# Vision layer on one core: image 0 of h is loaded at the end of the token stage, from a ring kept beside the constants

## The chip, the cores and the metric

The kernel is one launch on one core of a Trainium2 chip. The time is the device time of that core in microseconds (us), the median of several executions. Engines: TensorE (PE in the profile; PEld is its weight load), VectorE (DVE), ScalarE (ACT), GpSimd (POOL) and SyncE (SP, which here only issues transfers). Each engine works through its own list in order; semaphores tie the lists together. SP and ACT issue transfers whose descriptors hardware makes; those of POOL are made by software on POOL and put in a scratch area of on-chip memory (SBUF).

## The reference

Cut to what is computed (16 images, 256 tokens each, width 192):

```python
h = tok(x)                              # x [16,3,64,64]
#   three levels p = 1, 2, 4: patches in Hilbert order (a gather), 16 at a time,
#   o_p = patches @ W_p.T + b_p;  levels 2 and 4 interpolated to 256 tokens
#   h = concat(o_1, o_2, o_4) @ Wf.T + bf
h = h + attn(layernorm(h))              # 12 heads of 16, causal
#   q, k, v = layernorm(h) @ w_inp + b_inp
#   qf = (exp(q@omega - diag - max over features) + eps) / 8       (kf: max over heads, features)
#   a = (causal qf . kf . v) / (causal qf . kf + eps);  attn = a @ w_out + b_out
h = h + ffn(layernorm(h))               # 8 experts, 2 chosen by each token
#   probs = softmax(x @ gate_w + gate_b); y = sum over 2 of gelu(x @ w1_e + b1_e) @ w2_e + b2_e
#   + bk_scale * (clip(Green's function of x @ v_w) @ out_w + out_b)
```

## The kernel before

The kernel is three blocks, one after the other. A block has one instruction list for each engine, and the engines meet at its end before the next begins.

**Token stage** (`tokens_block`, 0 to about 84 us). POOL gathers the patches with 42 indirect transfers (L194); PE turns and multiplies them in groups, and DVE and ACT copy the even and the odd groups out of PSUM. The last work is h itself: for each half t of the tokens (t = 0, 1) eight groups of two images, ("h", 8t + n). Their results stand in `hs`. For each quarter q of the images SP waits for its two groups and stores half t of four images to the DRAM tensor `h_dram` (L179), eight stores of 384 KB. The four stores of t = 0 count on the semaphore `h_out[0]`, those of t = 1 on one each, `h_out[1]` to `h_out[4]`. So image 0 is whole in DRAM when all stores of t = 0 and the one of t = 1, q = 0 have landed. After its last store SP has nothing to wait for that is still open, and the block ends.

**Attention stage** (`attention_block`, about 84 to 429 us). The sixteen images go through a pipeline of four steps (`sched`): step `one` of image i, with steps of images i-1, i-2 and i-3 beside it. h of an image is read from `h_dram` into a ring `hb` of four places (192 KB an image, `load_h`, L473), counted by `h_in`. SP's list begins with the waits for `h_out[0]` and `h_out[1]` and with `load_h(0)`; then, for image i, it waits until image i has landed, issues `load_h(i + 1)`, and issues a sixteenth of the second expert weights (`a_raw`, L489). DVE's list begins with `stats1(0)` and `apply1(0)`: the sums of the first layer norm (L831, L834), a wait for POOL's reciprocal root (L519, L521), and the norm applied (L839). POOL's begins with four memsets (L508 to L513). PE's first instruction is the turn of the normed image (L576); ACT copies it out (L797), and the projections follow (L623 and L684). The order of all of this is written out by hand.

**Experts stage** (`experts_block`, about 429 us to the end). For 39 tiles of 256 slots POOL gathers token rows (L1141, 78 transfers) and adds the weighted results into the output (L1153, 78 transfers); eight transfers at the end add the spectral part (L1161). Its constants and the three weight tensors live beside the blocks in SBUF, so their places in memory depend on what stands before them.

Of the kernel before, what the change touches and what calls it, by code (L numbers as in the profile page):

```python
# [25 lines left out]
P = 128  # L26
B, T, D = 16, 256, 192
NT = B * T // P
TJ = T // P
KH = D // 2  # L30
# [7 lines left out]
NE, FF = 8, 768  # L38
# [32 lines left out]
def tokens_block(nc, a, keep, c, h_dram, x2_dram, tbl_dram):  # L71
# [6 lines left out]
    with ExitStack() as ctx:  # L78
        sb = lambda n, s, d=F32: ctx.enter_context(nc.sbuf_tensor("t_" + n, s, d))
# [67 lines left out]
        @block.sync  # L147
        def _(sp):
            sp.dma_start(idx[:], a["idx"].bitcast(U32)).then_inc(idx_in, 16)
            for dst, src in ((w2[:], a["w2"]), (w1[:], a["w1"]), (bias[:], a["tok_b"]), (up2[:], a["up2"]),  # L150
                             (wf02[0:EMB], a["wf"][0:EMB]), (wf02[EMB:P], a["wf"][2 * EMB:]),
                             (wf1[0:EMB], a["wf"][EMB:2 * EMB]), (wf1[EMB:EMB + 1], a["bf"])):
                sp.dma_start(dst, src).then_inc(params_in, 16)
            sp.dma_start(top[0:EMB], a["w0_b0"].unsqueeze(1).broadcast_to([EMB, B, EMB])).then_inc(top_in, 16)
            sp.dma_start(fine[EMB:P], a["up1"].unsqueeze(1).broadcast_to([EMB, B, T])).then_inc(up1_in, 16)
            sp.wait_ge(pads_ready, 3)
            sp.dma_start(tbl_dram.rearrange("(p n) c -> p (n c)", p=P), pads[:].rearrange("p n c -> p (n c)")).then_inc(pads_out, 16)
            sp.dma_start(x2_dram[B * T:].rearrange("(j p) c -> p j c", j=2), no_row[:].unsqueeze(1).broadcast_to([P, 2, XW])).then_inc(pads_out, 16)
            of_expert = lambda rows, e: a["ew1"][rows, 2 * e:2 * e + 2].rearrange("k u f -> k (u f)")
            for e in range(NE):  # L160
                if e == RING:
                    sp.wait_ge(omega_zero, 1)
                    for h in range(HC):
                        sp.dma_start(omega[h * NF:(h + 1) * NF, h, 0:NF], a["omega_t"]).then_inc(att_in, 16)
                    sp.dma_start(wqk_t, a["wqk_t"]).then_inc(att_in, 16)
                    for dst, src in ((c["wqkv"][:, :, 2 * H * HW:], a["wv"]), (c["w_out"][:], a["w_out"]), (c["w_gate"][:], a["w_gate"])):
                        for rows in (slice(0, KH), slice(KH, KH + 1)):
                            sp.dma_start(dst[rows], src[rows]).then_inc(att_in, 16)
                if e >= RING:
                    sp.wait_ge(w1_low, 2 * (e - RING + 1))  # L170
                sp.dma_start(raw_a[:, e % RING], of_expert(slice(0, P), e)).then_inc(raw_in[e % RING], 16)
                for r in (0, EMB):
                    sp.dma_start(raw_b[r:r + EMB, e % RING], of_expert(slice(P, D), e)).then_inc(raw_in[e % RING], 16)
            h_half = h_dram.rearrange("p b (j d) -> p b j d", j=TJ)
            for t in range(TJ):
                for q in range(B // 4):
                    b = slice(4 * q, 4 * q + 4)
                    wait_out(sp, ("h", 8 * t + 2 * q), ("h", 8 * t + 2 * q + 1))
                    sp.dma_start(h_half[:, b, t], hs[:, b, t]).then_inc(h_out[1 + q if t else 0], 16)  # L179
            sp.wait_ge(pads_out, 32)  # L180

        @block.gpsimd
# [201 lines left out]
def attention_block(nc, a, keep, c, h_dram, out, x2_dram, tbl_dram):  # L384
# [11 lines left out]
    with ExitStack() as ctx:  # L396
# [6 lines left out]
        eps_col, eight, region, minus_half, entry = (c[n] for n in ("eps_col", "eight", "region", "minus_half", "entry"))  # L403
        wqkv, w_out, w_gate, h_out = c["wqkv"], c["w_out"], c["w_gate"], c["h_out"]

        hb = sb("hb", [P, 4, TJ, D])
        stats, mv, rstd1 = sb("stats", [P, TJ, 6]), sb("mv", [P, TJ, 2]), sb("rstd1", [P, TJ])
        var_eps = {n: sb("var_eps_" + n, [P, TJ]) for n in ("rstd1_ready", "rstd2_ready")}
        xn = sb("xn", [P, TJ, D])
# [30 lines left out]
        AB = ps("ab", [P, 512])  # L440
        M = ps("misc", [P, 512])

        names = """setup h_in xn_ready xnT_done xnT_out qk_done v_done v_out top_done shift_done
            feat_raw exp_done hi_ready lo_ready qT_done kT_done qf_done qT_out kT_out qf_out state_done state_out
            s_done s_out av_done att_ready attT_done attT_out proj_done h2_ready xn2_ready xn2T_done xn2T_out logit_done
            logit_out found gap_ready prob_ready picked chosen_ready counted slots_ready prefix_done place_step rows_ready
            scattered h2_stored x2_stored cleared tail rstd1_ready rstd2_ready norm_step att_step
            raw_in high low""".split()
        s = {n: sem("b_" + n) for n in names}
        block = ctx.enter_context(nc.Block())  # L450
        SPARE = 4 * P - 2 * VW

# [17 lines left out]
        @block.sync  # L470
        def _(sp):
            def load_h(b):
                sp.dma_start(hb[:, b % 4], h_dram[:, bass.ds(b, 1)].rearrange("p b (j d) -> p (b j) d", j=TJ)  # L473
                             ).then_inc(s["h_in"], 16)

            def emit(i, one, two, tail, choice):
                if one and not (fixed(i) and i == B - 1):
                    if not fixed(i) or i >= 3:
                        sp.wait_ge(s["h2_stored"], 16 * (i - 2))
                        sp.wait_ge(s["xn2_ready"], i - 2)  # L480
                    sp.wait_ge(s["h_in"], 16 * (i + 1))
                    if fixed(i) and i == 3:
                        for q in range(1, B // 4):
                            sp.wait_ge(h_out[1 + q], 16)
                    load_h(i + 1)
                if one:
                    if not (fixed(i) and i == 0):
                        wait_apart(sp, s["low"], i)
                    sp.dma_start(raw[:], a["ew2"][:, bass.ds(i, 1)].rearrange("k u f d -> k (u f) d")).then_inc(s["raw_in"], 16)  # L489
                if tail:  # L490
                    wait_apart(sp, s["h2_ready"], i - 1)
                    sp.dma_start(out_tokens[bass.ds(i - 2, 1)].rearrange("b p j d -> (b p) j d"),
                                 hb[:, (i + 2) % 4]).then_inc(s["h2_stored"], 16)
                    wait_apart(sp, s["xn2_ready"], i - 1)
                    rows = x2_tokens[bass.ds(i - 2, 1)].rearrange("b p j d -> (b p) j d")
                    sp.dma_start(rows[:, :, 0:D], xn2[:]).then_inc(s["x2_stored"], 16)
                    sp.dma_start(rows[:, :, D:XW], xn2[:, :, P:D]).then_inc(s["x2_stored"], 16)
            sp.wait_ge(h_out[0], 16 * (B // 4))
            sp.wait_ge(h_out[1], 16)
            load_h(0)  # L500
            sched(sp, emit)
            sp.wait_ge(s["h2_stored"], 16 * B)
            sp.wait_ge(s["x2_stored"], 32 * B)
# [988 lines left out]
def vit_layer(nc, a, out):  # L1492

    scratch = lambda n, shape: nc.dram_tensor(n, shape, F32).ap()
    h_dram = scratch("h_dram", (P, B, TJ * D))
    x2_dram, tbl_dram = scratch("x2_dram", (B * T + TW, XW)), scratch("tbl_dram", (NSLOT, 2))
    v_dram, g_dram, spec_dram = scratch("v_dram", (NT, P)), scratch("g_dram", (2, B, T)), scratch("spec_dram", (B * T, D))
    with ExitStack() as ctx:
        sb = lambda n, s: ctx.enter_context(nc.sbuf_tensor(n, s, F32))
        ident_r = ctx.enter_context(nc.sbuf_tensor("ident", [P, P], F32R))  # L1500
        count = ctx.enter_context(nc.sbuf_tensor("count", [P, TJ, NE], BF16))
        pot = sb("pot", [P, B, TJ])
        w1 = {n: ctx.enter_context(nc.sbuf_tensor("x_" + n, [P, UNITS, UF], F32R)) for n in ("w1h", "w1l", "w1s")}
        w2s = ctx.enter_context(nc.sbuf_tensor("x_w2s", [P, UNITS, UT, 2 * D], F32R))
        keep = dict(ident_r=ident_r, count=count, pot=pot, w2s=w2s, **w1)
        with ExitStack() as inner:
            sb = lambda n, s, d=F32: inner.enter_context(nc.sbuf_tensor("c_" + n, s, d))
            c = dict(causal=sb("causal", [P, P], BF16), before=sb("before", [P, P], BF16), ones=sb("ones", [P, P], BF16),
                     block_mask=sb("block_mask", [HC * NF, HC, VW], BF16), own_head=sb("own_head", [HC * NF, 2]),
                     eps_col=sb("eps_col", [P, 1]), eight=sb("eight", [P, NE]), region=sb("region", [P, NE]),  # L1510
                     minus_half=sb("minus_half", [P, TJ]), entry=sb("entry", [P, 2, TJ, 2]),
                     wqkv=sb("wqkv", [KH + 1, 2, 2 * H * HW + D]), w_out=sb("w_out", [KH + 1, 2, D]),
                     w_gate=sb("w_gate", [KH + 1, 2, NE + 1]),
                     h_out=[inner.enter_context(nc.semaphore(f"h_out{n}")) for n in range(1 + B // 4)])
            tokens_block(nc, a, keep, c, h_dram, x2_dram, tbl_dram)
            attention_block(nc, a, keep, c, h_dram, out, x2_dram, tbl_dram)
        experts_block(nc, a, keep, x2_dram, tbl_dram, out, v_dram, g_dram, spec_dram)
# [53 lines left out]
```

## Time and profile before

| | us |
|---|---|
| median of 3 runs (812.67, 813.17, 816.4) | 813.17 |
| the profiled execution | 815.63 |
| its span, first to last instruction | 813.8 |
| PE busy | 675.7 (83%) |
| DVE busy | 499.9 (61%) |
| ACT busy | 438.0 (54%) |
| POOL busy | 437.3 (54%) |
| mean granted PE clock | 0.903 |

The profiled execution lies 2.46 us above the median, inside the range of the three runs. Times in a row are microseconds from the start of the span. In a timeline row the first number is the start, the second the length; a merged row (x2, x8) spans several instructions. In brackets stands how long the engine had been idle and what ended that. "PEclk" is the clock that was granted to PE as a share of 2.4 GHz: 1.00 is 2.4 GHz, 0.50 is 1.2 GHz.

### The profile page before, as it was taken

How to read it: one execution, taken by the hardware profiler on the slowest of the kernel's cores; microseconds unless marked ns; L12 is line 12 of the kernel's file. 1: busy time of each engine (PE TensorE's matmuls, PEld its weight loads, DVE VectorE, ACT ScalarE, POOL GpSimd, SP SyncE). 2: the span in 40 equal slices, each digit the busy share in tenths (PEclk: the TensorE clock that was granted, in tenths of full speed). 3: DMA queues.
4: the chain of work that ended last, by engine and by line, in shares of the span. 5: the costliest groups of instructions: out<-in, count | busy, mean ns of one | idle time of the engine just before them, and what ended most of it. 6: DMA issues, size and time to landing. Idle time of an engine off the chain costs nothing. (4 is left out here: it accounts for less than half of the span.)

```text
span 813.8 us, 17136 instructions
## 1 busy us (share of the span) xinstructions
PE 675.7 (83%) x4943; PEld 630.0 (77%) x4944; DVE 499.9 (61%) x1474; ACT 438.0 (54%) x852; POOL 437.3 (54%) x456
## 2 busy tenths in 40 slices
PE   2558489999999999999711899999979999999940
PEld 2328379988898999989611899999979999999940
DVE  1444337777777777776314588887996656656510
ACT  1334246766666666665001677767645665666610
POOL 7771223544555555444234377777765765665442
PEclk9659769999999999999555999999989999999985
DMA  8963302211221223210002143333322343343228
GB/s 206 224 137 98 104 25 55 56 49 47 47 57 47 60 57 61 47 37 24 24 23 45 32 68 56 60 61 57 63 39 47 68 74 77 76 76 78 50 39 155
DMA packets 63713, 55.08 MB, mean 68 GB/s; under 512 B 24345, under 2 KB 55520, under 8 KB 63664
## 3 DMA queue, kind: packets, MB, share of 16 engines
q0 software_dynamic: 19840, 23.53, 17.0%
q1 hardware_dynamic: 39344, 27.76, 14.7%
q10 hardware_dynamic: 4480, 3.21, 1.2%
q8 instruction: 21, 0.34, 0.2%
q14 instruction: 28, 0.23, 0.1%
HBM read 32.52 MB, written 25.10 MB: 71 GB/s over the span
## 5 line engine op out<-in xcount | busy, mean ns | idle before, releaser
L1153 POOL DMA_INDIRECT result<-e_y,e_tag x78 | 139.7, 1791 | 92.8 <-DVE e_y L1483 81.0
L1212 PE MATMUL e_yp<-x_w2s,e_hh 128*128 x468 | 140.9, 368 | 2.3 <-DVE e_y L1483 2.3
L1476 DVE TENSOR_TENSOR e_hl<-e_hid,e_hh 128x512 fp32r<-128x512 f32 x117 | 80.2, 690 | 90.4 <-ACT e_hh L1278 90.2
L534 POOL DMA_INDIRECT tbl_dram<-c_entry,a_slot x64 | 64.4, 1007 | 131.9 <-DVE c_entry L999 112.1
L1270 ACT ACTIVATE e_hid<-e_hidden,e_b 128x256 f32<-128x256 f32 x234 | 101.3, 475 | 54.0 <-PE e_hidden L1199 42.3
L1213 PE MATMUL e_yp<-x_w2s,e_hl 128*128 x468 | 118.2, 253 | 0.0
L616 PEld LDWEIGHTS a_ab<-a_values,a_masked 128*128 128x128 f32 x768 | 98.4, 199 | 13.8 <-issue 13.0
L616 PE MATMUL a_ab<-a_values,a_masked 128*128 (+1 forms) x768 | 103.9, 279 | 5.0 <-DVE a_masked L877 5.0
L1278 ACT CAST e_hh<-e_hid 128x512 fp32r<-128x512 f32 x117 | 72.4, 621 | 62.0 <-PE e_yp L1213 62.0
L1141 POOL DMA_INDIRECT e_x<-x_dram,e_tag x78 | 82.9, 1062 | 40.1 <-issue 21.0
L1212 PEld LDWEIGHTS e_yp<-x_w2s,e_hh 128*128 128x128 f32 x468 | 88.8, 190 | 2.6 <-issue 2.5
L1213 PEld LDWEIGHTS e_yp<-x_w2s,e_hl 128*128 128x128 f32 x468 | 90.5, 193 | 0.0
L1195 PE MATMUL e_hidden<-e_xh,e_w 128*128 128x256 f32 x234 | 73.0, 312 | 15.7 <-DVE e_xl L1347 12.0
L877 DVE TENSOR_TENSOR a_masked<-a_s,c_causal 128x512 f32<-128x512 f32 x96 | 64.6, 684 | 16.4 <-PE a_s L592 15.1
L1197 PE MATMUL e_hidden<-e_xl,e_w 128*128 128x256 f32 x234 | 67.4, 288 | 0.0
L1196 PE MATMUL e_hidden<-e_xh,e_w 128*128 128x256 f32 x234 | 67.4, 288 | 0.0
L1198 PE MATMUL e_hidden<-e_xh,e_w 128*128 128x256 f32 x234 | 67.3, 288 | 0.0
L1199 PE MATMUL e_hidden<-e_xl,e_w 128*128 128x256 f32 x234 | 67.2, 287 | 0.0
L1195 PEld LDWEIGHTS e_hidden<-e_xh,e_w 128*128 128x128 f32 x234 | 45.9, 196 | 20.2 <-issue 13.4
L788 ACT ACTIVATE a_qb_t<-a_fa,c_own_head 96x768 fp32r<-96x768 f32 x64 | 53.9, 893 | 6.8 <-PE a_fa L636 6.8
L527 POOL TENSOR_TENSOR a_split<-a_feat,a_split 128x192 fp32r<-128x192 f32 x64 | 36.6, 591 | 31.6 <-ACT a_split L773 30.3
L623 PE MATMUL a_fa<-c_wqkv,a_xn_t 97*128 97x408 f32 (+1 forms) x128 | 52.6, 535 | 0.9 <-ACT a_xn_t L797 0.9
(250 smaller groups left out, 1545.8 us busy)
## 6 DMA issues: line engine op xcount, KB each, us to landing
a_raw<-in_ew SPq DMA_DIRECT2D x16, 288.0 KB, 3.1
x_w2s<-in_ew SPq DMA_DIRECT2D x8, 384.0 KB, 11.8
x_w2s<-in_ew SPq DMA_DIRECT2D x16, 192.0 KB, 13.1
h_dram<-x_w2s SPq DMA_DIRECT2D x8, 384.0 KB, 2.7
a_hb<-h_dram SPq DMA_DIRECT2D x16, 192.0 KB, 3.4
result<-a_hb SPq DMA_DIRECT2D x16, 192.0 KB, 3.7
x_dram<-a_att SPq DMA_DIRECT2D x16, 192.0 KB, 3.7
spec_dram<-e_space ACTq DMA_DIRECT2D x16, 192.0 KB, 1.9
```

The lines of the kernel that those rows point to most:

```text
L616: last = pe.matmul(beside(o + r * VW), masked[n % 2][:, r], own_and_zeros.unsqueeze(1).broadcast_to([P, 2, 2, VW]), start=n == 0 and r == ...
L1141: pool.indirect_dma_start(out=x[:, i % 2, j], out_offset=None, in_=x2_dram, in_offset=bass.IndirectOffsetOnAxis(ap=tag[:, i % 8, j, 0:1].b ...
L1153: pool.indirect_dma_start(out=out, in_=y[:, j], in_offset=None, out_offset=bass.IndirectOffsetOnAxis(ap=tag[:, i % 8, j, 0:1].bitcast(U32) ...
L1195: pe.matmul(o, w(0), xh[:, 0], start=True, stop=False)
L1196: pe.matmul(o, w(1), xh[:, 0], start=False, stop=False)
L1197: pe.matmul(o, w(0), xl[:], start=False, stop=False)
L1198: pe.matmul(o, w(2), xh[:, 1], start=False, stop=False)
L1212: pe.matmul(Y[:, j, 0:2 * D], hh[:, f, c], w(f, 2 * D), start=f == 0, stop=False, skip_group_check=True)
L1213: last = pe.matmul(Y[:, j, 0:D], hl[:, f, c], w(f, D), start=False, stop=False, skip_group_check=True)
L1270: act.activation(hid[:, f], HID[:, f % 4, f // 4], ACT.Gelu_apprx_tanh, bias=b1[:, bass.ds(e, 1), f]).then_inc(s["hid_ready"], 1)
L1278: act.copy(hh[:, f:f + 2].rearrange("p f t -> p (f t)"), hid[:, f:f + 2].rearrange("p f t -> p (f t)")).then_inc(s["hid_high"], 1)
L1476: g.tensor_tensor(hl[:, f:f + 2].rearrange("p f t -> p (f t)"), hid[:, f:f + 2].rearrange("p f t -> p (f t)"), hh[:, f:f + 2].rearrange("p ...
```

## The change

`hb` and the semaphore `h_in` move from the attention stage to the tensors that both stages share (`c`). In the token stage SP, after the store of t = 1, q = 1, waits for `h_out[0]` and `h_out[1]` and issues the load of image 0; the stores of q = 2 and q = 3 follow behind it. The same two waits and the load go from the head of the attention stage. The ring now takes 6 KB of each partition during the token stage too; the scratch for POOL's descriptors is set to 8192 bytes of a partition, half of the 16384 that it has without the argument.

```diff
@@ tokens_block, SP @@
                     wait_out(sp, ("h", 8 * t + 2 * q), ("h", 8 * t + 2 * q + 1))
                     sp.dma_start(h_half[:, b, t], hs[:, b, t]).then_inc(h_out[1 + q if t else 0], 16)
+                    if t and q == 1:
+                        sp.wait_ge(h_out[0], 16 * (B // 4))
+                        sp.wait_ge(h_out[1], 16)
+                        sp.dma_start(c["hb"][:, 0], h_half[:, 0]).then_inc(c["h_in"], 16)
             sp.wait_ge(pads_out, 32)
@@ attention_block @@
-        hb = sb("hb", [P, 4, TJ, D])
+        hb = c["hb"]
...
-        names = """setup h_in xn_ready ...
+        names = """setup xn_ready ...
         s = {n: sem("b_" + n) for n in names}
+        s["h_in"] = c["h_in"]
...
-            sp.wait_ge(h_out[0], 16 * (B // 4))
-            sp.wait_ge(h_out[1], 16)
-            load_h(0)
             sched(sp, emit)
@@ vit_layer @@
-                     w_gate=sb("w_gate", [KH + 1, 2, NE + 1]),
+                     w_gate=sb("w_gate", [KH + 1, 2, NE + 1]), hb=sb("hb", [P, 4, TJ, D]),
+                     h_in=inner.enter_context(nc.semaphore("h_in")),
@@ kernel @@
-    nc = bacc.Bacc("TRN2", target_bir_lowering=False, num_devices=1)
+    nc = bacc.Bacc("TRN2", target_bir_lowering=False, num_devices=1, dynamic_dma_scratch_size=8192)
```

On SP's list the end of the token stage and the head of the attention stage stand thus before (L179 the stores of h, L78 the end of the block, L473 the loads of h, L489 the expert weights):

```order
L179 DMA h_dram<-x_w2s 128x4x192 x8
L78 UNCONDITIONAL_BRANCH
L470 UNCONDITIONAL_BRANCH
L473 DMA a_hb<-h_dram 128x384 x2
L489 DMA a_raw<-in_ew 128x576
L473 DMA a_hb<-h_dram 128x384
L489 DMA a_raw<-in_ew 128x576
```

And now, at the same place on SP (L183 is the new load, L478 and L494 are the old L473 and L489):

```order
L179 DMA h_dram<-x_w2s 128x4x192 x6
L183 DMA c_hb<-h_dram 128x384
L179 DMA h_dram<-x_w2s 128x4x192 x2
L78 UNCONDITIONAL_BRANCH
L475 UNCONDITIONAL_BRANCH
L478 DMA c_hb<-h_dram 128x384
L494 DMA a_raw<-in_ew 128x576
L478 DMA c_hb<-h_dram 128x384
L494 DMA a_raw<-in_ew 128x576
```

One load has moved from behind the block's end to between the sixth and the seventh store; of the two loads that stood at the head of the attention stage one is left. The lists of the other four engines are the same, line numbers apart.

## Rows read from the trace of the kernel before

**Rows 1.** Waits from 84 to 120 us: engine, line, releaser; total us, times, longest.

```profile
PE a_fa L576 <- DVE a_xn L839: 7.2, 1, 7.2
```

**Rows 2.** Timeline, all engines, from the block's start to the projections.

```profile
84.13 0.07 DVE L826 MEMSET count<- 128x8 uint32 x1 [0.92 <-PEq L78]
...
86.72 0.62 DVE L831 BATCH_NORM_STATS2 a_stats<-a_hb 128x6 f32<-128x192 f32 x2 [2.53 <-DMA a_hb<-h_dram]
...
87.88 0.24 POOL L519 TENSOR_SCALAR a_var_eps_rstd_ready<-a_mv 128x2 f32<-128x2 f32 x1 [2.44 <-DVE a_mv L834]
...
89.85 1.06 PE L576 MATMUL a_fa<-ident,a_xn 128*96 128x128 f32 x4 [7.24 <-DVE a_xn L839]
...
91.43 0.67 ACT L799 CAST x_w2s<-a_raw 128x576 fp32r<-128x576 f32 x1
...
91.58 3.09 PE L623 MATMUL a_fa<-c_wqkv,a_xn_t 96*128 96x408 f32 x4 [0.67 <-ACT a_xn_t L797]
```

**Rows 3.** Timeline of SP, each issue by itself.

```profile
79.33 0.37 SPq L179 DMA_DIRECT2D h_dram<-x_w2s  x1
80.63 0.37 SPq L179 DMA_DIRECT2D h_dram<-x_w2s  x1
81.94 0.37 SPq L179 DMA_DIRECT2D h_dram<-x_w2s  x1
83.24 0.37 SPq L179 DMA_DIRECT2D h_dram<-x_w2s  x1
84.13 0.36 SPq L473 DMA_DIRECT2D a_hb<-h_dram  x1
86.65 0.36 SPq L473 DMA_DIRECT2D a_hb<-h_dram  x1
87.05 0.43 SPq L489 DMA_DIRECT2D a_raw<-in_ew  x1
```

**Rows 4.** All instructions of line 179, the stores of h: time to landing.

```profile
DMA to landing us min/median/max: 2.7/2.7/4.0
```

**Rows 5.** All instructions on tile a_hb, its 16 loads among them: time to landing.

```profile
DMA to landing us min/median/max: 2.0/3.6/5.4
```

**Rows 6.** Windows: us, busy time of PE, PEld, DVE, ACT, POOL, PEclk, share and GB/s of DMA.

```profile
80.00:80.50 0.50, 0.50 (x6) 0.50 (x4) 0.45 (x1) 0.00 (x0) 0.00 (x0) 1.00 0.43 151
...
86.00:86.50 0.50, 0.00 (x0) 0.00 (x0) 0.00 (x0) 0.00 (x0) 0.00 (x0) 0.84 0.26 93
```

**Rows 7.** Windows of 1 us in the attention stage's start, where the clock changes.

```profile
96.00:97.00 1.00, 1.00 (x5) 1.00 (x5) 0.40 (x1) 0.00 (x0) 0.00 (x0) 0.71 0.00 0
100.00:101.00 1.00, 0.04 (x1) 0.07 (x1) 0.85 (x5) 0.86 (x2) 1.00 (x3) 0.50 0.00 0
...
117.00:118.00 1.00, 1.00 (x9) 1.00 (x8) 0.87 (x2) 0.31 (x1) 0.00 (x0) 0.97 0.00 0
```

**Rows 8.** Timeline: ACT's last use of gathered data; PE's projections of images 0 and 2.

```profile
74.29 0.58 ACT L379 COPY x_w2s<-t_g 128x384 f32<-128x384 f32 x1
...
94.47 2.51 PE L684 MATMUL a_fb<-c_wqkv,a_xn_t 96*128 96x192 f32 x8
...
132.19 1.53 PE L623 MATMUL a_fa<-c_wqkv,a_xn_t 96*128 96x408 f32 x4
133.56 1.47 PE L684 MATMUL a_fb<-c_wqkv,a_xn_t 96*128 96x192 f32 x8
```

**Rows 9.** Line 194, POOL's gathers: ns min/median/max, first and last start; landing.

```profile
L194 POOL DMA_INDIRECT t_g<-in_x,t_idx x42: 951/955/1712, 3.0 to 60.9; - x42
...
DMA to landing us min/median/max: 2.3/6.1/9.3
```

**Rows 10.** Transfers from 780 us to the end: packets, MB, share; then the issues.

```profile
q0 software_dynamic: 1728, 3.54, 61.9%
...
result<-spec_dram POOLq DMA_DIRECT2D x8, 384.0 KB, 9.9
result<-e_y,e_tag POOLq DMA_INDIRECT x4, 3.5
```

More of the change, by code:

```diff
@@ L441, in attention_block @@
         M = ps("misc", [P, 512])
-        names = """setup h_in xn_ready xnT_done xnT_out qk_done v_done v_out top_done shift_done
+        names = """setup xn_ready xnT_done xnT_out qk_done v_done v_out top_done shift_done
             feat_raw exp_done hi_ready lo_ready qT_done kT_done qf_done qT_out kT_out qf_out state_done state_out
```

## The prediction

> **What bounds the kernel now.** The page's summary first: PE is busy 83% of the span, so whatever leaves PE idle for some microseconds is paid in full, unless it is hidden in a wait that another engine causes. The change sits at the seam of token and attention stage, so the waits of that stretch come next [rows 1]. The longest of PE there is 7.2 us before L576, for DVE's normed image 0. The timeline shows what is behind it, one chain without slack [rows 2]: DVE is free at 84.20 (84.13 + 0.07), waits 2.53 us for the transfer that brings image 0, sums from 86.72; POOL takes the root from 87.88; DVE applies; PE turns at 89.85; ACT copies; PE projects from 91.58. Each link starts when the one before ends, no other input is late. So the time at which h of image 0 lands sets the start of the whole attention pipeline.
>
> When does it land? SP's issues [rows 3]: the last store at 83.24, the load at 84.13 once the blocks have changed, and at 86.65 the next load, which had waited for the landing. The load took 86.65 - 84.13 = 2.52 us. It needed neither the block's end nor the last two stores: image 0 was complete with the store of 79.33, which lands 2.7 us later (median and minimum, 4.0 at most) [rows 4], at 82.03.
>
> **The load, moved.** Nothing is added or taken away in transfers; one 192 KB load goes past two stores and past the block's end. Step by step on SP: the store of q = 1 goes at 80.63 as before and ends at 81.00. SP then waits for the landing of the store of 79.33, to 82.03; the four stores of t = 0 were issued before that one, in the same queue, and have landed by then too. The load is issued at about 82.05. With the 2.52 us that the same load took before, it lands at 84.57; with the least that any load of h took, 2.0 [rows 5], at 84.05; with the most, 5.4, at 87.45. Which is nearest? The data of the four stores and the load ran from about 80.2 to 86.1 (the half microseconds at both ends are busy to 0.43 and 0.26) [rows 6]: 5.9 us for 4 x 384 + 192 = 1728 KB, so 1.3 us for a store and 0.7 for the load, 0.9 us from the first issue (79.33) to its data, 0.5 us from the load's last data to its landing (86.65). Now the second store's data end at about 80.2 + 2.6 = 82.8, the load's run from 82.95 (82.05 + 0.9) to 83.6, and it lands at 84.1. I take 84.35, the middle of this and 84.57.
>
> DVE cannot start before 84.20, its memset's end, so 86.72 - 84.20 = 2.5 us is the most that can be won. POOL had been idle for 2.44 us when it took the root at 87.88 [rows 2], so it allows 2.44. With the landing at 84.35 DVE starts at 84.4: **gain 2.3 us**. With 84.57 it is 2.1; with the slowest load a loss of 0.8 (87.5 against 86.72).
>
> **What queues behind the new wait.** On SP the store of q = 2 stands behind it: it went at 81.94 [rows 3] and would go at 82.45, 0.5 us late. The last store, due at 83.24, is reached at 82.8 and goes on time; the block's end waits for SP's issue of it, not for its landing (issued at 83.24, attention begins at 84.13), so the end does not move. If instead the awaited store takes 4.0 us (82.03 becomes 83.33), the load goes at 83.35, the last two stores at 83.7 and 84.1, SP ends 0.9 us later than now and so does the block: the load then lands at 85.4 to 85.9 (2.0 to 2.52) and the gain is 0.8 to 1.3. The stores of q = 2 and 3 are first wanted for images 8 and up, far later. In the attention stage SP's head is shorter: the load of image 1 goes at 84.4 in place of 86.65 and the expert weights at 84.8 in place of 87.05 [rows 3], behind the last stores' data (to about 86.1 still, as nothing is added). The cast of these weights comes at 91.43 [rows 2], moving to 89.1; that leaves 4.3 us after the issue, about what it had (4.4). Nothing there is late. After that every wait of the pipeline is relative to its own chain, so I let 2.3 us pass to the end undiminished.
>
> **The clock.** PE falls idle at 82.61 (89.85 - 7.24) and its clock falls to 1.2 GHz between 86.0 and 86.5 (the mean of 0.84 puts it near 86.3) [rows 6]. It is back at 2.4 GHz between 96 and 97, falls again at 100 and returns at 117 [rows 7]. The idleness becomes 7.2 - 2.3 = 4.9 us, from 82.6 to 87.5, and takes in the time of the fall still; I let the clock fall as before. What a stretch at the low clock costs: L623 four times 3.09 against 1.53, L684 eight times 2.51 against 1.47 [rows 2, 8], so 1.56 + 1.04 = 2.6 us for one image's projections. The change shifts the work by 2.3 us against whatever times the clock; that is worth something between plus and minus 2.6 and I take it at nothing. [...]
>
> **The scratch and the places in SBUF.** Both are costed at nothing. Bounds: the most transfers of POOL in flight are the closing eight (median 9.9 us to landing) and the gathers (6.1 us, one every (60.9 - 3.0) / 41 = 1.41 us, so 4 to 5 at a time, 7 at the slowest landing) [rows 9, 10]. 12 transfers made 1728 packets, 144 each, 9 on each of 16 engines; eight make 72. The trace does not show how many the scratch holds; below nothing there is no reason for a gain. [...]
>
> **The sum.** The profiled execution took 815.63, span 813.8 and 1.83 around it. Its own sum: 815.63 - 2.3 = 813.3. It lies 2.46 above the median of the runs; taken from that median, 813.17 - 2.3 = **810.9 us**.
>
> **Rivals.**
> *The clock pays too.* With 4.9 us of idleness for 7.2, PE is at the high clock for one image's projections that ran low: 2.3 + 2.6 = 4.9, 808.3 us. For it: the fall at 86.3 comes only in the second half of the present idleness, and the clock's later turns at 96 to 97 and at 100 are close to each other, so that a shift could merge or drop one. Against: PE works but 0.04 us between 100 and 101 and the clock was down there as well [rows 7], after less idleness than the 4.9 us that remain here. 12 in 100.
> *The gain is taken back.* The load lands as late as the slowest of the 16, or the store before it takes 4.0, or the clock stays low over one more image's projections (2.3 gained, 2.6 lost: 813.5). The first two give a loss of 0.8 (814.0) and a gain of 0.8 (812.4); I name 813.2 us. For it: in the loop the median load takes 3.6, which here would leave 1.1. Against: what is queued ahead is less than before. 25 in 100.
> *The halved scratch is too small (slower).* POOL must wait for landings before it can write further descriptors. It decides from the point where fewer than four gathers fit. With three, each takes 6.1 / 3 = 2.03 us in place of 1.41: 41 x 0.62 = 25 us; the last gather lands at 60.9 + 6.1 = 67.0 and is used at 74.29 [rows 8], so 7.3 are free and 18 remain: 810.9 + 18 = 829 us. With four (1.53 each, 5 us) the slack covers it. For it: only the argument's value; against: with twice the room no gather issue took over 1.71 us [rows 9], and 4 x 9 packets is little. 5 in 100.
>
> **Chances.** Forecast (load hidden, clock as before) 58, the clock pays too 12, gain taken back 25, scratch 5. 0.5% is 4.1 us, about what a measurement of this kernel can tell from no change: faster means under 809.1, slower over 817.2. Only the clock's case and a few of the forecast's executions are under: 13 in 100. The scratch alone is over: 5. The rest, 82, is within. The likeliest case has 809.3 to 812.8 for itself (gain 0.8 to 2.5, and a clock term of about 1.3 either way). The range takes in the clock's case and the taken-back gain with the spread of the runs: 808.0 to 814.5; it leaves out the scratch and the outermost clock phases.
>
> **What would show it right or wrong.** Right: on SP an issue of the load at about 82.05 between two stores; DVE's wait before L831 gone or under 0.3 us, L831 at 84.3 to 84.6, L576 at 87.5, PE's wait before it 4.9; block's start still at 84.1; the start of the experts stage 2.3 us earlier but for the clock; the POOL gathers at 0.95 us and the last at 60.9 as before. Wrong: DVE's first instruction later than 84.3 (SP held the block's end), a load that took over 3 us (stores in its way), gathers of more than 1.8 us (scratch), or a clock trace with other turns between 86 and 117: then the difference is not the load's.

## The result and the profile after

| | before | after |
|---|---|---|
| median, us (6 runs each) | 813.91 | 804.57 |
| all runs | 812.67, 813.17, 816.4, 812.33, 821.01, 814.66 | 804.63, 804.19, 805.36, 809.46, 804.34, 804.51 |
| profiled execution, its span | 815.63, 813.8 | 804.63, 802.8 |
| PE, DVE, ACT, POOL busy, us | 675.7, 499.9, 438.0, 437.3 | 672.7, 500.8, 438.2, 437.5 |

The ratio is 0.9882 [0.9839, 0.9925]: 9.3 us less by the medians, four times the 2.3 us that were forecast, and below the range. The two profiled executions lie 11.0 us apart, so the stretches below add up to that. In some of the runs below the token stage took 10 to 26 us longer than in before (the kernel before lay mostly at 817 to 846 us beside them, once at 1187), so those totals can't tell 2 to 5 us, and only the stretches behind A are read. The busy times of the two hardly differ (PE's fell by 3.0 us, with a mean clock of 0.911 for 0.903), so most of the time came out of idleness. To see where, both traces are cut at the same landmarks. A is DVE's first memset of the attention stage; S the first sums (L831, after L833); B the last of the 64 scatters of slots (L534, after L536); C POOL's first memset of the experts stage (L1118, after L1120); D the first weighted add (L1153, after L1155); F the first closing transfer (L1161, after L1163).

| us | to A | A to S | S to B | B to C | C to D | D to F | F to end |
|---|---|---|---|---|---|---|---|
| before | 84.13 | 2.59 | 334.02 | 8.28 | 35.96 | 326.84 | 21.98 |
| after | 82.34 | 0.64 | 334.27 | 4.23 | 34.90 | 325.83 | 20.59 |
| difference | -1.79 | -1.95 | +0.25 | -4.05 | -1.06 | -1.01 | -1.39 |

F to end is rounded to the span's tenth. One of the seven stretches is the one that the forecast spoke of (A to S). The largest, B to C, lies at the other end of the attention stage.

**The load.** The timeline of after at the block's start, with the rows that answer to [rows 2]; before the bracket start, length, engine, line and operation, in the bracket the idle time and its releaser:

```profile
82.34 0.07 DVE L828 MEMSET count<- 128x8 uint32 x1 [0.91 <-PEq L78]
...
82.98 0.62 DVE L833 BATCH_NORM_STATS2 a_stats<-c_hb 128x6 f32<-128x192 f32 x2 [0.57 <-DMA c_hb<-h_dram]
...
84.13 0.24 POOL L521 TENSOR_SCALAR a_var_eps_rstd_ready<-a_mv 128x2 f32<-128x2 f32 x1 [0.48 <-DVE a_mv L836]
...
86.11 1.06 PE L578 MATMUL a_fa<-ident,a_xn 128*96 128x128 f32 x4 [5.27 <-DVE a_xn L841]
```

SP's issues in the same trace, against [rows 3]:

```profile
77.56 0.37 SPq L179 DMA_DIRECT2D h_dram<-x_w2s  x1
78.86 0.37 SPq L179 DMA_DIRECT2D h_dram<-x_w2s  x1
80.28 0.36 SPq L183 DMA_DIRECT2D c_hb<-h_dram  x1
80.73 0.42 SPq L179 DMA_DIRECT2D h_dram<-x_w2s  x1
81.46 0.37 SPq L179 DMA_DIRECT2D h_dram<-x_w2s  x1
82.90 0.36 SPq L478 DMA_DIRECT2D c_hb<-h_dram  x1
```

The store that is waited for went at 77.56, the load at 80.28 (2.7 us), and the next load, which waits for its landing, at 82.90: the load took 2.62 us. DVE's 2.53 us of waiting became 0.57, and POOL's 2.44 became 0.48.

**The end of attention.** POOL's last scatter and first memset of the experts stage, first before, then after. The number in the second row's bracket is what counts:

```profile
420.74 0.95 POOL L534 DMA_INDIRECT tbl_dram<-c_entry,a_slot  x1 [0.30 <-issue]
429.02 0.31 POOL L1118 MEMSET e_wide<- 128x256 f32 x1 [7.32 <-POOLq L396]
```

```profile
417.25 0.96 POOL L536 DMA_INDIRECT tbl_dram<-c_entry,a_slot  x1 [0.30 <-issue]
421.48 0.31 POOL L1120 MEMSET e_wide<- 128x256 f32 x1 [3.27 <-POOLq L400]
```

The windows of that idle time (columns as in [rows 6]), before and after:

```profile
422.00:422.50 0.50, 0.00 (x0) 0.00 (x0) 0.00 (x0) 0.00 (x0) 0.00 (x0) 0.50 0.05 2
422.50:429.00 6.50, 0.00 (x0) 0.00 (x0) 0.00 (x0) 0.00 (x0) 0.00 (x0) 0.50 0.00 0
```

```profile
418.50:419.00 0.50, 0.00 (x0) 0.00 (x0) 0.00 (x0) 0.00 (x0) 0.00 (x0) 0.50 0.05 2
419.00:421.40 2.40, 0.00 (x0) 0.00 (x0) 0.00 (x0) 0.00 (x0) 0.00 (x0) 0.50 0.00 0
```

The last scatter's packets are in the first window of each pair (2 GB/s); in the second no packet moves and no engine is busy, for 6.5 us before and 2.4 us after. The rows of the line of the block's end (L396 before, L400 after) show where the engines are: ACT, SP, PE and DVE come to it between 414.6 and 416.3 us before (411.0 and 412.8 after), and their last row there, the semaphore, is at 428.9 (421.4), after a DRAIN that POOL's sequencer executes from 423.5 (420.5) and of which the windows above show nothing. In its row stand the length in ns (least, median, most) and the start in us, before and after:

```profile
L396 POOLq DRAIN  x1: 5285/5285/5285, 423.5 to 423.5; - x1
```

```profile
L400 POOLq DRAIN  x1: 712/712/712, 420.5 to 420.5; - x1
```

The DRAIN is 4.57 us shorter, and 0.26 us after it POOL starts on the next block, in both. The 0.5 us between this and the stretch's 4.05 lie ahead of the DRAIN: 2.73 us from the last scatter to it before, 3.26 after, and 2.7 to 3.5 in all profiles of this document, with no order by scratch (2.7 at 8192 in e1 as at 16384 in before). There are three such ends. At that of the token stage the DRAIN takes 3.50 us in both kernels, but from 64.6 us on before (66.2 after), while SP comes to that end at 83.7 (81.9 after). The last one closes the kernel, before and after:

```profile
L1017 POOLq DRAIN  x1: 3159/3159/3159, 810.4 to 810.4; - x1
```

```profile
L1019 POOLq DRAIN  x1: 1852/1852/1852, 800.7 to 800.7; - x1
```

That is 1.31 of the 1.39 us of the closing stretch. What the change touches and what is in use at these ends is POOL's scratch, and the places of the tensors.

### The profile page after: what moved, and what is told of

The parts are those of the page before. It is cut to its first block and busy times, and to the rows that moved or that the text cites. A ratio compares the mean times of both kernels' runs of the same rounds, so it can differ in the third digit from the quotient of the medians.

```text
span 802.8 us, 17136 instructions
## 1 busy us (share of the span) xinstructions
PE 672.7 (84%) x4943; PEld 626.9 (78%) x4944; DVE 500.8 (62%) x1474; ACT 438.2 (55%) x852; POOL 437.5 (55%) x456
## 5 line engine op out<-in xcount | busy, mean ns | idle before, releaser
L1155 POOL DMA_INDIRECT result<-e_y,e_tag x78 | 138.3, 1773 | 94.6 <-DVE e_y L1485 82.7
L536 POOL DMA_INDIRECT tbl_dram<-c_entry,a_slot x64 | 64.5, 1008 | 132.9 <-DVE c_entry L1001 99.1
L1197 PE MATMUL e_hidden<-e_xh,e_w 128*128 128x256 f32 x234 | 72.1, 308 | 17.2 <-DVE e_xl L1349 12.5
L1201 PE MATMUL e_hidden<-e_xl,e_w 128*128 128x256 f32 x234 | 66.5, 284 | 0.0
L1198 PE MATMUL e_hidden<-e_xh,e_w 128*128 128x256 f32 x234 | 66.4, 284 | 0.0
L1199 PE MATMUL e_hidden<-e_xl,e_w 128*128 128x256 f32 x234 | 66.4, 284 | 0.0
L1200 PE MATMUL e_hidden<-e_xh,e_w 128*128 128x256 f32 x234 | 66.4, 284 | 0.0
```

The costliest lines, as they stand in the source:

```text
L1155: pool.indirect_dma_start(out=out, in_=y[:, j], in_offset=None, out_offset=bass.IndirectOffsetOnAxis(ap=tag[:, i % 8, j, 0:1].bitcast(U32) ...
L1197: pe.matmul(o, w(0), xh[:, 0], start=True, stop=False)
L1198: pe.matmul(o, w(1), xh[:, 0], start=False, stop=False)
L1199: pe.matmul(o, w(0), xl[:], start=False, stop=False)
L1200: pe.matmul(o, w(2), xh[:, 1], start=False, stop=False)
L1201: pe.matmul(o, w(2), xl1[:], start=False, stop=True).then_inc(s["hid_done"], 1)
```

## The experiments

In short, what all runs gave. "Pending" is the count that the theory named P2 below gives at the end of attention; the DRAIN columns are POOL's, at the end of attention and at the kernel's end.

| run | scratch, bytes | moved load | DVE's wait | pending | DRAIN | POOL idle before experts | DRAIN at the end | F to end |
|---|---|---|---|---|---|---|---|---|
| before | 16384 | no | 2.53 | 64 | 5.29 | 7.32 | 3.16 | 21.98 |
| after | 8192 | yes | 0.57 | 8 | 0.71 | 3.27 | 1.85 | 20.59 |
| e1_scratch_only | 8192 | no | 2.6 | 8 | 0.72 | 2.74 | 1.85 | 20.89 |
| e2_scratch_same_places | 8192 | no | 2.6 | 8 | 0.71 | 3.30 | 1.85 | 20.88 |
| e12_scratch_only_5r | 8192 | no | 2.6 | 8 | 0.71 | 2.87 | 1.85 | 20.80 |
| e16_scratch_only | 8192 | no | 2.6 | 8 | 0.71 | 3.18 | 1.85 | 20.56 |
| e13_changed_again | 8192 | yes | 0.54 | 8 | 0.71 | 2.95 | 1.85 | 20.70 |
| e3_load_only | 16384 | yes | 0.54 | 64 | 5.29 | 7.60 | 3.16 | 22.31 |
| e11_load_only_5r | 16384 | yes | 0.54 | 64 | 5.29 | 7.52 | 3.16 | 21.93 |
| e15_load_only | 16384 | yes | 0.58 | 64 | 5.29 | 7.74 | 3.16 | 22.08 |
| e5_scratch_14336 | 14336 | no | 2.6 | 64 | 5.29 | 7.54 | 4.30 | 23.24 |
| e6_scratch_12288 | 12288 | no | 2.6 | 64 | 5.29 | 7.54 | 4.30 | 23.52 |
| e9_scratch_9728 | 9728 | no | 2.6 | 64 | 5.29 | 7.59 | 3.16 | 22.14 |
| e10_scratch_8960 | 8960 | no | 2.6 | 2 | 0.22 | 2.27 | 3.00 | 21.89 |
| e8_half_scatters | 16384 | no | 2.6 | 32 | 2.67 | 5.05 | 3.16 | 21.95 |
| e7_scratch_4096 | 4096 | yes | 0.6 | 8 | 0.71 | 2.75 | 1.28 | 20.07 |
| e14_scratch_4096_5r | 4096 | yes | 0.7 | 8 | 0.71 | 2.94 | 1.28 | 20.11 |
| e4_scratch_2048 | 2048 | yes | 0.7 | 8 | 0.72 | 3.54 | 0.42 | 22.42 |

**Each half of the change alone.** The kernel before with `dynamic_dma_scratch_size=8192` as its only edit:

```diff
-    nc = bacc.Bacc("TRN2", target_bir_lowering=False, num_devices=1)
+    nc = bacc.Bacc("TRN2", target_bir_lowering=False, num_devices=1, dynamic_dma_scratch_size=8192)
```

> The kernel before with the scratch halved to 8192 bytes and nothing else. Theory S (the scratch sets how long POOL takes at a block's end): POOL idle before the experts stage falls from 7.3 to about 3.3 us, the stretch from the last data to the span's end from 4.2 to about 2.9 us; total about 5.5 us faster than before, near 808.4 us. Theory C (the clock's timing made the difference beyond the load's 2 us): both stretches as before, 7.3 and 4.2, total unchanged within 1 us, near 813.9. Theory A (the tensors' places in SBUF): as S in total; the next run tells them apart.

The total, 834.8 against 830.16, ratio 1.0058 [1.0000, 1.0117], does not show the gain that theory S expected; A is at 108.2 us, 24 us later than in before, so it decides nothing. But B to C is 3.70 for 8.28, with POOL idle for 2.74:

```profile
449.37 0.31 POOL L1118 MEMSET e_wide<- 128x256 f32 x1 [2.74 <-POOLq L396]
```

The same with 8 KB of each partition left unused in front of the first tensor, so that every tensor stands where it stood before:

```diff
+        sb("kept_free", [P, 2048])
```

> As the run before, and 8192 bytes of each partition stay unused in front of all tensors, so every tensor stands where it stood in the kernel before. Theory S: same as the run before, near 808.4, POOL idle 3.3 us. Theory A (places): all is as in the kernel before, 813.9 and 7.3 us.

B to C is 4.26, F to end 20.88, and both DRAINs are as short as in e1: places in SBUF have no part in it. The other half, the changed kernel with the scratch of before; room for the ring is made by laying the token stage's small tensors (pads, row numbers, two weights, indices) into it:

```diff
+        free = c["hb"][:].rearrange("p n j d -> p (n j d)")
...
+                        sp.wait_ge(pads_out, 32)
                         sp.wait_ge(h_out[0], 16 * (B // 4))
```

> The load moved as in the changed kernel, the scratch left at 16384 bytes; room comes from placing pads, pad_id, no_row, wf02, w1 and idx of the token stage in the ring's own memory (SP waits for pads_out before the load, long passed). Load's own worth 2.0 us (DVE's wait 2.53 to 0.57). Theory S: POOL idle stays 7.3 and the end 4.2; total about 2 us under before, 811.9. Theory C: the earlier start shifts the clock favourably, total about 9 us under before, 804.6.

A to S is 0.61, B to C is back at 8.56. First DVE's wait, then POOL's:

```profile
110.39 0.62 DVE L839 BATCH_NORM_STATS2 a_stats<-c_hb 128x6 f32<-128x192 f32 x2 [0.54 <-DMA c_hb<-h_dram]
...
454.85 0.31 POOL L1126 MEMSET e_wide<- 128x256 f32 x1 [7.60 <-POOLq L406]
```

The total, 834.75 and 1.0076 [1.0022, 1.013], again with A 26 us late, decides nothing either. By the stretches the load owns A to S, and the scratch owns the two DRAINs in B to C and F to end.

**What the scratch does at a block's end.** Two theories at first: F, that POOL goes through the whole scratch, so the time grows with its size; and P, that it goes through the transfers not yet struck off, the 42 token gathers among them, which changes at a size in between.

> The kernel before with 14336 bytes of scratch. The stretch from the last table scatter's issue to the experts stage was 8.3 and 8.6 us with 16384 bytes, 3.7 and 4.3 with 8192, 4.5 with 2048. Theory F (grows with the size): 7 to 8 us here. Theory P (POOL goes at the block's end through the transfers that it has not struck off yet; it strikes off finished ones when the scratch is full, and 9 descriptors of 16 bytes for each of 106 transfers, 15264 bytes, fit in 16384 and in nothing here smaller): 3.7 to 4.5 us.

> The kernel before with 12288 bytes of scratch. Theory F: 6 to 7 us from the last table scatter to the experts stage. Theory P: 3.7 to 4.5 us. From the first closing add to the span's end, 22.0 and 22.3 us at 16384 and 20.6 to 20.9 at 8192: F 21.4, P depends on where the scratch was last full and may lie anywhere between.

Both gave 7.54 us:

```profile
428.55 0.31 POOL L1118 MEMSET e_wide<- 128x256 f32 x1 [7.54 <-POOLq L396]
```

F falls (it wanted less at 12288 than at 16384; the DRAIN is 5.29 us at 16384, 14336, 12288 and 9728), and so does P in the form in which the token stage's gathers count. What is left, P2: each block begins with none pending, a transfer stays pending until the scratch is full, and then all that have landed are struck off at once. It says that fewer scatters cost less at an unchanged scratch:

```diff
-                    store_slots(0)
...
-            pool.wait_ge(s["scattered"], 16 * 4 * B)
+            pool.wait_ge(s["scattered"], 16 * 2 * B)
```

This leaves out half of the 64 scatters, so the experts' part of each image's first token half is missing from the output.

> The kernel before, 16384 bytes of scratch, without the table scatters of the first half of each image's tokens (32 scatters instead of 64; these table entries stay at their pads, so the tokens get no expert's part). Theory P: with 74 transfers instead of 106 (or 32 instead of 64) not struck off, the extra 4.3 us of the last stretch (8.3 against 4.0) falls to 2.2 to 3.0, so 6.1 to 7.0 us. Theory F: 8.3 us. Theory W (it is the passing of the end of the scratch or a threshold of transfers): 4.0 or 8.3 us, nothing between.

```profile
420.80 0.31 POOL L1117 MEMSET e_wide<- 128x256 f32 x1 [5.05 <-POOLq L396]
```

B to C is 6.01, a little under the 6.1 to 7.0 expected. The DRAIN alone, in which no packet moves (none from 417.5 to 420.8 us), is 5.29 - 2.67 = 2.62 us shorter for 32 scatters fewer: 0.082 us each. P2 has a sharp edge, too. The sizes for it were taken over: if a scatter counts as 9 on an engine, as the transfers of [rows 10] do, and each of the 9 takes 16 bytes of a partition, 64 scatters fill 64 x 9 x 16 = 9216 bytes. The trace of before confirms neither (the last four scatters have 128 packets there, 2 for each on an engine), so the runs have to. Just above 9216 bytes, P2 says, nothing is struck off before the end, just below nearly all.

> The kernel before with 9728 bytes of scratch, 608 descriptors of 16 bytes. 16384, 14336 and 12288 bytes all gave 8.3 to 8.6 us from the last table scatter to the experts stage, half the scatters 6.0, 8192 and less 3.7 to 4.5. Theory P2 (POOL goes through the transfers issued since the last block's end and not yet struck off, 64 with 9 descriptors each, 576; the scratch is never full if it holds 576): 8.3 to 8.6 us. Theory T (some other threshold between 8192 and 12288): open.

> The kernel before with 8960 bytes of scratch, 560 descriptors, 16 fewer than the 576 of theory P2. P2: the scratch is full at the 63rd of the 64 scatters, the finished ones are struck off, 3.7 to 4.3 us. If the count of descriptors is not 9 for each, or the 42 gathers of the token stage count as well, it stays at 8.5.

9728 bytes first, then 8960:

```profile
450.94 0.31 POOL L1118 MEMSET e_wide<- 128x256 f32 x1 [7.59 <-POOLq L396]
```

```profile
433.79 0.96 POOL L534 DMA_INDIRECT tbl_dram<-c_entry,a_slot  x1 [2.86 <-issue]
435.06 0.96 POOL L534 DMA_INDIRECT tbl_dram<-c_entry,a_slot  x1 [0.30 <-issue]
438.28 0.31 POOL L1118 MEMSET e_wide<- 128x256 f32 x1 [2.27 <-POOLq L396]
```

7.59 against 2.27 us idle, 5.29 against 0.22 us of DRAIN; B to C is 3.23, under the 3.7 to 4.3 expected. The first of the three rows shows a pause where P2 puts the striking off: it is the 63rd scatter, the first for which 9 x 63 x 16 = 9072 bytes exceed 8960, and POOL pauses 2.86 us before it where its neighbours have 0.30. Here that gives half of the gain back. With 8192 bytes the 57th should pause (9 x 57 x 16 = 8208), and it does. The 57th in before, which waits for DVE's table, and in after:

```profile
404.44 0.96 POOL L534 DMA_INDIRECT tbl_dram<-c_entry,a_slot  x1 [12.98 <-DVE c_entry L999]
```

```profile
402.28 0.96 POOL L536 DMA_INDIRECT tbl_dram<-c_entry,a_slot  x1 [14.02 <-issue]
...
413.46 0.96 POOL L536 DMA_INDIRECT tbl_dram<-c_entry,a_slot  x1 [5.36 <-DVE c_entry L1001]
```

The idle time is 1.04 us longer there (1.7 in e1, e2, e12, e13 and e16), and the 61st (last row) again waits 5.36 us for DVE, as in before: the pause is gone in POOL's spare time. So it costs little at 8192 bytes; S to B is 334.4 to 335.0 us in e1, e2, e12 and e16, against 333.5 to 334.0 in before, e5 and e6.

**How small can it be.** The rival "scratch too small" was tried with the changed kernel at a quarter and at an eighth.

> The changed kernel with 4096 bytes of scratch. Both theories: 3.7 to 4.5 us from the last table scatter to the experts stage. Closing adds: at 2048 the last was issued 16.8 us after the first (POOL waited for room), at 8192 after 4.0 us. If a transfer takes 9 descriptors of 16 bytes, 4096 bytes hold 28, and the eight adds go out in 4 us and end in 20.7 us; if room is still short, 22 us as at 2048.

> The changed kernel with 2048 bytes of scratch. Theory S, time goes with the scratch's size: the block-end stretches shrink further, POOL idle before the experts stage to 1.5 to 2.5 us, the end to 2 us; total 801 to 803. Rival R (too small a scratch makes POOL wait for landings): gather and scatter issues above 2 us or gaps between them, the eight closing adds issued over more than 7 us; total 805 to 830.

With 4096 bytes: 802.62 in one run (815.66 for the kernel before beside it). 28 scatters fit by P2, so the 29th should pause as well, and it does, 7.93 us where in after it waits 7.17 us for DVE's table:

```profile
271.44 1.06 POOL L536 DMA_INDIRECT tbl_dram<-c_entry,a_slot  x1 [7.93 <-issue]
```

B to C is 3.71, D to F 325.43, F to end 20.07. S to B is 331.29, 3.0 us less than in after; the clock differs there, below. With 2048 (822.67 against 830.16, ratio 0.9973 [0.9918, 1.0029]) D to F is 328.64 for 325.83 and S to B 337.87 for 334.27. POOL is idle for 3.54 us before the experts stage, not for the 1.5 to 2.5 of theory S: what counts is what is pending, and with 8 pending the DRAIN is as long as at 8192 (0.72 and 0.71 us). At the end POOL seems to have no room for the last of the eight adds:

```profile
793.94 6.03 POOL L1163 DMA_DIRECT2D result<-spec_dram  x7 [2.32 <-DMA result<-e_y,e_tag]
810.71 0.81 POOL L1163 DMA_DIRECT2D result<-spec_dram  x1 [10.74 <-issue]
```

It stands for 10.74 us with nothing recorded that it waits for. The DMA engines are busy all the while until a point between 809 and 810 (a share of 1.14 in 808 to 809, 0.72 in the next, 0.00 in 810 to 811), and the eighth goes at 810.71: it fits a wait for the landings of the seven. So a wait like the rival's shows, two halvings below the change.

**Totals.** Each half once more, then the whole change, then 4096 bytes.

> The load moved, scratch 16384, timed again, since the first timing lay on a chip whose token stage took 20 us longer and scattered. Load's worth by the traces 2.0 us: ratio 0.9975. Theory C (the load brings more by the clock): 0.99.

> The scratch halved, the load where it was, timed again. By the traces 4.0 to 4.6 us before the experts stage and 1.1 to 1.4 at the end, 5.5 us: ratio 0.993. If the two add, load and scratch make 7.5 of the 9.3 us measured.

> Load moved, scratch 16384 bytes. By the stretches 2.0 us: 812.0 against 814.0, ratio 0.9975. If it were 0.99 the load would carry more than its stretch shows.

> Scratch 8192 bytes, load where it was. By the stretches 4.0 to 4.6 and 1.1 to 1.4 us: 808.5 against 814.0, ratio 0.993. The sum of the two, 7.5 us, against 7.5 to 9.3 measured of the whole change.

Load alone: 1.0021 [0.9979, 1.0063] and 1.0117 [1.0011, 1.0222]. Scratch alone: 0.9866 [0.9786, 0.9946] and 1.0021 [0.9901, 1.0141]. The kernel before lay at 833.27 and 837.89 beside them, and A is at 97 to 107 us in all four profiles. The halves could not be timed by their totals; the stretches behind A say once more what they said (A to S 0.61 and 0.64 with the moved load, 2.69 and 2.66 without; B to C 8.48 and 8.70 with 16384, 3.83 and 4.14 with 8192). Three of the four totals lie above 1. The intervals of e3, e11 and e15 exclude what their stretches give (1.95 us, a ratio of 0.998), that of e1 excludes 0.993, and only e12 shows a gain. For the moved load at 16384 a part of that may be real: the variant lays tensors of the token stage into the ring and waits for the pads, and an effect of a few microseconds ahead of A can't be told from the scatter there. It would belong to the variant, which the change is not. No total shows what either half is worth alone.

> The changed kernel once more. If the 1.8 us of the token stage belong to the change, attention begins 1.8 us earlier than in an undisturbed before (84.1) again; if they are chance, anywhere from 82.3 to 84.1, as kernels with the old token stage have shown (84.13, 83.90, 82.30, 82.89). Waits: before L833 0.6 us; last table scatter to experts 3.7 to 4.3 us; closing stretch 20.6 to 20.9 us. Ratio to before 0.988 to 0.992.

> The changed kernel with 4096 bytes, beside the one with 8192. By theory P2 at about 72 ns for each transfer not struck off: as with 8192 before the experts stage (3.7), the closing stretch 20.1 in place of 20.7 us; total 0.5 to 1 us faster than with 8192. If POOL's waits for room cost anything, the stretch of the experts' tiles (325.4 to 326.4 us in all others) grows.

Here the totals lie close together (812.33 to 815.74 in 11 runs of the kernel before). The changed kernel: 806.54 against 814.05, ratio 0.9905 [0.9884, 0.9926], so 7.5 us. The stretches that the change owns give 1.95 + 4.05 + 1.39 = 7.4. The block's start in its profile:

```profile
84.21 0.07 DVE L828 MEMSET count<- 128x8 uint32 x1 [0.91 <-PEq L78]
84.82 0.62 DVE L833 BATCH_NORM_STATS2 a_stats<-c_hb 128x6 f32<-128x192 f32 x2 [0.54 <-DMA c_hb<-h_dram]
```

A is at 84.21, as in before. The profiled execution took 820.25, and its S to B is 344.68, ten more than in after. Nearly all of it is there before the first scatter (73.7 us behind S, 64.0 in after), and the clock shows why: it fell at 110 and stayed low to 140, through work that ran at the high clock in after. The same window in after and in e13:

```profile
117.00:130.00 13.00, 12.25 (x103) 11.38 (x103) 8.06 (x21) 8.85 (x15) 4.58 (x7) 1.00 0.08 24
```

```profile
117.00:130.00 13.00, 12.64 (x60) 11.66 (x58) 4.89 (x14) 5.15 (x9) 4.53 (x7) 0.50 0.09 23
```

PE executed 60 multiplies there in place of 103. The two profiles with 4096 bytes show the opposite: the clock fell at 99 (e7) and 103 (e14) and was back at 106 and 110, a low stretch of 6.8 us where before and after have 17.1; their first scatter is 60.1 us behind S, and S to B is 331.3. Attention issues no software transfer before its first scatter, so nothing shows that the scratch does this; e13, with 8192 bytes, had the same short low stretch (99 to 106) before the long one.

The changed kernel with 4096 bytes: 804.39 against the same 814.05, 0.9879 [0.9859, 0.9899]. It beats the kernel before, and is the lower of the two; its interval overlaps that of 8192, and so the 2 us between them stay unproved. The shorter DRAIN at the end (1.28 for 1.85) can account for 0.6 of them.

## Why the prediction was wrong, by its steps

**Load: mechanism right, size 1.95 for 2.3.** The awaited store took 2.7 us as forecast, the load 2.62 where 2.30 was taken (landing 84.35 after an issue at 82.05): of the two estimates the direct one, 2.52, was nearer, and the one from the data's run, 84.1, was too early. So DVE's wait kept 0.57 us where 0.2 were forecast. PE's wait before the turn is 5.27, forecast 4.9. The new wait did not hold SP's last store up: it goes 3.90 us after the awaited one (77.56 to 81.46), in before 3.91 (79.33 to 83.24), and A comes 0.88 and 0.89 us behind it. The relief did not shrink on its way: S to B is 334.02 and 334.27. One sum was wrong: with a gain of 0.8 and a clock term of 1.3 the likeliest case reaches up to 813.17 - 0.8 + 1.3 = 813.7, not 812.8; the range has room for it.

**Clock: taken at nothing, came to nothing in this pair, by luck.** The views give the clock as a share (0.50 to 1.00); the prediction's GHz stand in none of them, and nothing rests on them. It turns at other places. Windows of 1 us of after, against [rows 7]:

```profile
83.00:84.00 1.00, 0.00 (x0) 0.00 (x0) 0.84 (x4) 0.00 (x0) 0.59 (x2) 0.78 1.10 373
93.00:94.00 1.00, 1.00 (x4) 0.73 (x3) 0.00 (x0) 0.48 (x2) 0.00 (x0) 0.60 0.00 0
97.00:98.00 1.00, 0.53 (x4) 0.56 (x4) 0.57 (x4) 0.97 (x2) 1.00 (x2) 0.60 0.00 0
114.00:115.00 1.00, 1.00 (x7) 0.98 (x7) 0.38 (x1) 0.46 (x2) 0.00 (x0) 0.86 0.00 0
```

Down at 83 to 84, up at 93, down at 97, up at 114: each nearly 3 us earlier than before (114.3 for 117.1 by the means of the last windows), where the work is 3.7 earlier (82.98 for 86.72 at the first sums). Four turns before, four after, +0.25 us over the stretch. The rival in which the clock pays 2.6 us did not happen in after, but the clock can do as much: in e7 and e14 the stretch is 3.0 us shorter, and in e13 ten longer. So the term is one of the execution and not of the change, and its bound of 2.6 us was too small.

**The failed step: "The scratch and the places in SBUF. Both are costed at nothing ... below nothing there is no reason for a gain".** That was half right: the places are worth nothing (e2). How much the scratch holds the prediction could not read from its rows; the runs show it, 56 scatters in 8192 bytes, the 57th pauses, and 56 is far more than the 7 gathers at most and the 8 adds that it found in flight. But the scratch was asked only whether it has room for what is in flight. The runs show a second cost, which goes with the count of the transfers issued and, by P2, not yet struck off (5.29 us with 64, 2.67 with 32, 0.71 with 8, 0.22 with 2); it is paid in the DRAIN at the block's end, where in before the other four engines stand from 416.3 to 428.9 us. A smaller scratch moves it to where POOL has time (1.04 us at the 57th scatter in after, with 5.36 us of waiting for DVE before the 61st still left). Worth 4.57 us of DRAIN at the end of attention (5.29 to 0.71; the stretch B to C fell by 4.05, 8.28 to 4.23) and 1.31 at the kernel's end (3.16 to 1.85 in each run at 8192; the stretch fell by 1.1 to 1.4). The trace of before could have raised the question: no engine is busy and no packet moves in 422.5 to 429, and the rows of L396 have the DRAIN of 5.29 us. The prediction read the trace only at the seam where instructions moved, while the change had a second part that works wherever POOL issues transfers.

**The rest: chance.** To A there are 1.79 us between the profiles. With the old token stage A is at 84.13, 83.90, 82.30 and 82.89 (before, e5, e6, e8); with the new one at 82.34, 82.93, 84.21, 86.25 and 86.91 (after, e7, e13, e4, e14). The two sets overlap, so nothing shows that any of it is due to the change. In the two profiles the clock differs, low up to 62.5 us in before and high from 60 in after; that this makes the 1.79 us is likely and not shown (the same window of each, in this order):

```profile
60.00:61.00 1.00, 1.00 (x10) 0.74 (x8) 0.00 (x0) 0.14 (x1) 0.70 (x2) 0.50 0.16 25
```

```profile
60.00:61.00 1.00, 1.00 (x16) 0.87 (x14) 0.56 (x1) 0.20 (x1) 0.70 (x1) 1.00 0.23 25
```

C to D and D to F (2.1 us together) vary as much among the runs with one and the same scratch (34.90 to 38.04, 325.37 to 326.56 at 8192). So the stretches give the change 7.4 of the 9.3 us (the total of e13 has 7.5), and nothing shows that the rest is its work.

**Rival "gain taken back".** The awaited store did not take 4.0, nor the load 5.4. **Rival "scratch too small".** It needed the scratch at an eighth, not at half: at 2048 the last of the 42 gathers goes at 69.6 us (62.3 in after), less than the 25 us later that it named for a scratch of three gathers, and A is at 86.25.

## What to carry to other kernels

Where a setting changes something that is used in many places, look at every place that uses it, the ends of blocks first: ask who owns a window in which no engine and no DMA is busy; here the rows of the line at the block's end, with the sequencers' own instructions, said it (the DRAIN, 5.29 of 6.5 us). With software transfers from GpSimd, count how many a block issues between two ends and try a smaller scratch: here 4096 bytes were at least as good as 16384 (a ratio of 0.9879), and 2048 too little (10.74 us of pause before the last add). And where totals scatter, read the stretches between landmarks that both kernels have; they told 2 us apart in runs whose totals differed by 20 and more. But look at the clock in a stretch before its length is put down to the edit: here it went with 3 us less (e7, e14) and 10 us more (e13) of one stretch.

## What the runs showed of the hardware

- At the end of a block POOL's sequencer executes a DRAIN, and its length goes with the number of software transfers that P2 counts as pending: 5.29 us with 64, 3.50 with 42 (the token stage's gathers; 4.0 to 4.35 in e1, e3, e11 and e12), 2.67 with 32, 0.71 with 8, 0.22 with 2. That is a line, 0.06 us and 0.082 us for each. That POOL strikes transfers off, and that the DRAIN goes through the pending ones one by one, is inferred from this line and from the pauses; no row shows either. In the token stage at 4096 and 2048 bytes it took 1.38 and 0.23 us, which by the line stands for 16 and 2 pending, where the plain count of P2 leaves 14 in both; P2's count was borne out in attention only; why not there is open.
- A scatter of 128 rows takes 143.7 to 144.5 bytes of scratch in a partition, so 144: the scatter that pauses is the 57th at 8192 (8192 / 57 = 143.7) and the 63rd at 8960 (8960 / 62 = 144.5), the 29th and the 57th at 4096, and at 9728 none does. How the 144 divide, 9 x 16 or otherwise, no run shows. Such a pause within a block made POOL's idle time 0.8 to 2.6 us longer.
- F to end without its DRAIN is 18.7 to 19.2 us in every profile but that at 2048 (22.0), so the DRAIN is what the scratch changes there. Open: how many are pending at that point. The experts stage issues 167 transfers; of 144 bytes each they would leave 54 pending at 16384 and 55 at 8192, while the DRAIN's length stands for about 38 and 22.
- From one execution to the next the clock turned at different places of the same work: in the start of attention it was low for 10.2 us and back at 1.00 for 3.4 in all five profiles read there, and then low again for 17.1 us in before and after, for 6.8 in e7 and e14, and for 6.8 and then 30.7 in e13.
- Open: why PE stands still in some token stages. At 9728 bytes, where A is at 104.9 us, PE was idle for 2.2 us or more before seven multiplies of L262, with nothing recorded that they waited for and the DMA engines busy to 0.14 from 50 to 57 us. One of them:

```profile
54.16 0.58 PE L262 MATMUL tk<-x_w2s,t_w 48*64 48x256 f32 x1 [2.21 <-issue]
```
